# A reduction to tridiagonal form on one core: the gate ahead of the matrix product, the norm behind the panel factor, filled pauses, and direct products for 3-tile steps

## What is computed

```python
deg = jnp.sum(A, axis=0) + jnp.sum(A, axis=1) - jnp.diagonal(A)
d_inv_sqrt = jnp.where(deg > 0, jax.lax.rsqrt(deg), 0.0)
L_norm = d_inv_sqrt[:, None] * (jnp.diag(deg) - A) * d_inv_sqrt[None, :]
_, U = jnp.linalg.eigh(L_norm)
agg = jnp.einsum('mn,bnd->bmd', U.T, features)
h = jax.nn.relu(agg @ W1 + b1)
return jnp.einsum('nm,bmd->bnd', U, h @ W2 + b2)
```

## Time and profile before

| | us |
|---|---|
| median of 3 runs | 4991.18 (4988.99 to 4991.94) |
| the profiled execution | 4989.5 |
| its span, first to last instruction | 4987.7 |
| DVE busy | 4026.5 (81%) |
| PE busy | 2551.1 (51%) |
| ACT busy | 1139.3 (23%) |
| POOL busy | 284.9 (6%) |
| the 510 reduction steps, first reciprocal to last | 55.0 to 2527.7 |

### The profile page before, as it was taken

One profiled execution on the slowest core, in us unless ns is written; L12 is line 12 of the kernel. 1 busy time (PEld: TensorE's weight loads), 2 busy tenths in 40 slices (PEclk: granted clock), 3 DMA queues, 4 the chain that ended last, 5 costly groups with the idle time before them and its releaser, 6 DMA issues.

```text
span 4987.7 us, 116618 instructions
## 1 busy us (share of the span) xinstructions
PE 2551.1 (51%) x40168; PEld 1721.1 (35%) x40168; DVE 4026.5 (81%) x24921; ACT 1139.3 (23%) x5016; POOL 284.9 (6%) x1424
## 2 busy tenths in 40 slices
PE   4666666555556666544457645657423223135048
PEld 3444444444445555433322212322122223124024
DVE  7666666777777888888889999999967897988956
ACT  1212222222223333333311143333210200301001
POOL 1111111111110000000000000000000000000000
PEclk6555555555555555555567767778755555557579
DMA  2000000000000000000000000000000000000001
GB/s 69 2 2 2 2 2 2 2 2 2 2 2 3 4 4 4 3 3 2 3 1 1 1 1 1 1 1 1 1 1 0 0 0 0 0 0 1 0 0 34
DMA packets 20961, 20.11 MB, mean 4 GB/s; under 512 B 6544, under 2 KB 16784, under 8 KB 20368
## 3 DMA queue, kind: packets, MB, share of 16 engines
q1 hardware_dynamic: 20368, 12.65, 0.9%
HBM read 8.41 MB, written 4.20 MB: 3 GB/s over the span
## 4 chain that ended last, share of the span: by engine, by line
DVE 68%; PE 21%; issue 7%; ACT 2%; SPq 0%; DVEq 0%; DMA 0%; POOL 0%
PE bank L622 10%; DVE qp L1437 2%; DVE hid L1096 2%; DVE dif L1799 2%; PE bank L593 2%; PE bank L617 2%; DVE pcol L1076 2%; DVE tau_row L1084 2%; DVE qp L1424 2%; DVE gated L1082 2%; DVE ts L1040 1%; DVE yz L1055 1%; ACT ts L358 1%; DVE hid L1085 1%; PE bank L783 1%
## 5 line engine op out<-in xcount | busy, mean ns | idle before, releaser
L622 PE MATMUL bank<-lapw,hid 128*32 128x160 f32 (+3 forms) x10200 | 660.0, 420 | 81.5 <-DVE lapw L1105 58.3
L622 PEld LDWEIGHTS bank<-lapw,hid 128*32 128x32 f32 x10200 | 394.3, 162 | 200.0 <-DVE lapw L1105 79.7
L700 PE MATMUL bank<-hid,rows 128*128 128x512 f32 (+1 forms) x504 | 320.1, 802 | 275.3 <-ACT dif L410 271.9
L586 PE MATMUL bank<-xp,ones 128*32 128x1 f32 x4080 | 146.0, 202 | 458.1 <-DVE xp L1070 240.6
L371 ACT ACTIVATE swap<-vcols 128x4 f32<-128x4 f32 (+3 forms) x510 | 105.7, 207 | 1049.4 <-DVE xp L1070 696.8
L1050 DVE TENSOR_TENSOR yz<-bank,pick 128x128 f32<-128x128 f32 (+3 forms) x510 | 117.6, 231 | 233.7 <-PE bank L622 233.5
L700 PEld LDWEIGHTS bank<-hid,rows 128*128 128x128 f32 x504 | 118.7, 242 | 468.1 <-ACT dif L410 297.2
L586 PEld LDWEIGHTS bank<-xp,ones 128*32 128x32 f32 x4080 | 102.6, 140 | 501.4 <-DVE xp L1070 262.2
L593 PE MATMUL bank<-ycol,vcols 128*32 128x1 f32 x3064 | 89.8, 199 | 236.3 <-DVE ycol L1061 236.3
L593 PE MATMUL bank<-hid 128*32 128x1 f32 x3064 | 89.8, 199 | 191.6 <-DVE hid L1096 191.6
L586 PE MATMUL bank<-xn,ones 128*32 128x2 f32 x4080 | 141.2, 198 | 84.1 <-DVE xn L1009 84.1
(11 more groups left out here) (761 smaller groups left out, 8268.9 us busy)
## 6 DMA issues: line engine op xcount, KB each, us to landing
out_x<-xs SPq DMA_DIRECT2D x16, 256.0 KB, 2.5
lapw<-in_adj SPq DMA_DIRECT2D x1, 1024.0 KB, 5.3
bias_rows<-in_L_gnn_bg SPq DMA_DIRECT2D x8, 64.0 KB, 5.8
hid<-pair SPq DMA_DIRECT2D x32, 1.0 KB, 1.7
bias_rows<-in_L_gnn_b SPq DMA_DIRECT2D x4, 64.0 KB, 5.7
wg<-in_L_gnn_Wg SPq DMA_DIRECT2D x2, 64.0 KB, 4.8
wg<-in_L_gnn_W SPq DMA_DIRECT2D x2, 64.0 KB, 4.3
dif<-in_L_gnn_Wih SPq DMA_DIRECT2D x1, 0.5 KB, 7.1
```

The source lines that it names most:

```text
L586: m = pe.matmul(into[32 * q:32 * q + 32, :], weights, column, start=True, stop=True)
L622: m = pe.matmul(bank[1][32 * q:32 * q + 32, 0:(T + 1) * 32].rearrange("p (u i) -> p u i", i=32), acols[:, t, k:k + 1].to_broadcast([P, 32] ...
L700: m = pe.matmul(bank[4 * h + q][:, 0:cols_], wih_t[:, p - 1, q * P:(q + 1) * P], hid[:, b0:b0 + nb, t:t + (nw - 1) * p + 1:p], start=True, ...
```

## The change

Two predicates take the place of one. `gated_early(k)` holds for T of 4 and 3, `direct(k)` for T of 3, 2 and 1.

- **T of 4 and 3**: POOL's tail goes to PE in the middle of y, behind its second live tile, and no longer behind y. DVE computes the gate, `gated`, `tau_row`, `scrow` and `ats` ahead of its wait for y, and no longer behind `a1`. The factor (L1103 of before) comes ahead of the norm pair of the next step; the pair comes between the factor and the panel write, and raises one semaphore once instead of twice.
- **T of 3**: v.y and v.p are direct products on PE, 12 each, and the two reduces on DVE go.
- **T of 1**: the strips (and the slots) are issued in the pauses behind the pivot's factor and ahead of v.
- **All direct products**: the loops in `product` change places, the tile outside and the quarter inside.
- The wait for the pivot's value stands behind the reciprocal, and `pcol` has a semaphore of its own, for which ACT's `w0` and DVE's `bcol_` wait.

The diff, cut to its core:

```diff
-def dots(k):
-    return NT - (k + 1) // P <= DOT_TILES
+def gated_early(k):
+    return NT - (k + 1) // P >= 3
+
+
+def direct(k):
+    return NT - (k + 1) // P <= 3
...
@@ ACT
+                act.wait_ge(pcol_ready, k + 1)
                 act.activation(w0[:, t0:], pcol[:, t0:], ACT.Copy, scale=tau_row[:, k:k + 1]).then_inc(w0_ready, 1)
...
@@ PE
-                for q in range(4):
-                    for t in range(T):
+                for t in range(T):
+                    for q in range(4):
                         m = pe.matmul(into[32 * q:32 * q + 32, :], left[:, t:t + 1].to_broadcast([P, 32]), right[:, t:t + 1], start=(t == 0), stop=(t == T - 1))
...
+                    if t == t0 + 1 and early:
+                        pe.wait_ge(tail_in, k + 1)
+                        everywhere(bank[4][:, 0:1], ones[:, 0:32], xn[:, 2:3]).then_inc(tail_ps, 1)
                 m.then_inc(y_done, 1)
...
+                pe.wait_ge(x_ready, k + 1)
+                if direct(k):
                     product(bank[3][:, 0:1], vcols[:, t0:, k], ycol[:, t0:]).then_inc(vy_ps, 1)
-                    pe.wait_ge(x2_ready, k + 1)
+                    pe.wait_ge(pcol_ready, k + 1)
                     product(bank[2][:, 4 * NB:4 * NB + 1], vcols[:, t0:, k], pcol[:, t0:]).then_inc(vp_ps, 1)
...
@@ DVE
                 a = put(V.tensor_scalar(ts[:, 4:5], ts[:, 3:4], bank[0][:, 0:1], ts[:, 0:1], ALU.mult, ALU.add))
+                if T == 1:
+                    z = strips()
                 after(a)
                 a = put(V.tensor_tensor(pair[:, k, 0:1], ts[:, 4:5], ts[:, 1:2], ALU.mult))
                 b = put(V.scalar_tensor_tensor(pair[:, k, 1:2], ts[:, 4:5], ts[:, 1:2], alpha, ALU.mult, ALU.add))
+                if T == 1 and j:
+                    c = slots()
...
+                if early:
+                    dve.wait_ge(tail_ps, k + 1)
+                    g = put(V.tensor_scalar(gate_row[:, k:k + 1], bank[4][:, 0:1], 1e-24, -1.0, ALU.is_gt, ALU.mult))
+                    after(g)
+                    g = put(V.tensor_scalar(gated[:], inv[:], gate_row[:, k:k + 1], None, ALU.mult))
+                    after(g)
+                    V.tensor_tensor(tau_row[:, k:k + 1], gated[:, 0:1], gated[:, 1:2], ALU.mult).then_inc(p_ready, 1)
+                    dve.wait_ge(p_ready, k + 1)
+                    g = put(V.tensor_scalar(scrow[:, k:k + 1], tau_row[:, k:k + 1], gated[:, 0:1], -1.0, ALU.mult, ALU.mult))
+                    after(g)
+                    put(V.scalar_tensor_tensor(ats[:, t0:], a_, scrow[:, k:k + 1], ltm[:, t0:, k + 1], ALU.mult, ALU.mult))
+                if T > 1:
+                    z = strips()
+                    if j:
+                        c = slots()
+                after(z)
+                y = V.tensor_reduce(ycol[:, t0:], yz[:, t0:, 0:32 + 2 * j], AX.X, ALU.add)
...
-                dve.wait_ge(norm_ps, k + 1)
-                if k + 1 < STEPS and not dots(k + 1):
-                    norms(k + 1)
                 dve.wait_ge(vp_ps, k + 1)
                 dve.wait_ge(w0_ready, k + 1)
-                half = ts[:, 7:8] if dots(k) else tau_row[:, k:k + 1]
+                half = ts[:, 7:8] if direct(k) else tau_row[:, k:k + 1]
                 a = put(V.tensor_scalar(ts[:, 6:7], bank[2][:, 4 * NB:4 * NB + 1], tau_row[:, k:k + 1], half, ALU.mult, ALU.mult))
+                if gated_early(k + 1):
+                    dve.wait_ge(norm_ps, k + 1)
+                    norms(k + 1)
                 after(a)
```

More of the change, by code:

```diff
@@ L1024, in _ @@
                 v, a_ = vcols[:, t0:, k], acols[:, t0:, k]
[L1025 removed]
+                early = gated_early(k)
+                alpha = bank[0][:, 1:2] if early else bank[5][:, 0:1]
                 if j == 0 and k:
@@ L1043, in _ @@
                 b = put(V.scalar_tensor_tensor(pair[:, k, 1:2], ts[:, 4:5], ts[:, 1:2], alpha, ALU.mult, ALU.add))
+                if T == 1 and j:
+                    c = slots()
                 after(a)
-                vdone = put(V.scalar_tensor_tensor(v, onehot[:, t0:, k + 1], pair[:, k, 0:1], a_, ALU.mult, ALU.add))
+                put(V.scalar_tensor_tensor(v, onehot[:, t0:, k + 1], pair[:, k, 0:1], a_, ALU.mult, ALU.add))
                 after(b)
-                put(V.reciprocal(inv[:], pair[:, k, :]))
@@ L1059, in _ @@
-                after(a)
-                if dots(k):
-                    V.tensor_reduce(ycol[:, t0:], yz[:, t0:, 0:32 + 2 * j], AX.X, ALU.add).then_inc(x_ready, 1)
+                d = put(V.reciprocal(inv[:], pair[:, k, :]))
+                if early:
+                    dve.wait_ge(tail_ps, k + 1)
[8 more added lines that the diff above has]
+                    put(V.scalar_tensor_tensor(ats[:, t0:], a_, scrow[:, k:k + 1], ltm[:, t0:, k + 1], ALU.mult, ALU.mult))
@@ L1075, in _ @@
                     dve.wait_ge(w0_ready, k)
-                p = V.scalar_tensor_tensor(pcol[:, t0:], a1[:, t0:], pair[:, k, 0:1], ycol[:, t0:], ALU.mult, ALU.add)
-                if dots(k):
-                    p.then_inc(x2_ready, 1)
-                else:
-                    put(p)
-                after(g)
-                g = put(V.tensor_scalar(gated[:], inv[:], gate_row[:, k:k + 1], None, ALU.mult))
-                after(g)
-                V.tensor_tensor(tau_row[:, k:k + 1], gated[:, 0:1], gated[:, 1:2], ALU.mult).then_inc(p_ready, 1)
@@ L1085, in _ @@
-                b = put(V.scalar_tensor_tensor(bcol_[:, t0:, k + 1], pcol[:, t0:], gated[:, 0:1], a1[:, t0:], ALU.mult, ALU.add))
-                dve.wait_ge(p_ready, k + 1)
-                c = put(V.tensor_scalar(scrow[:, k:k + 1], tau_row[:, k:k + 1], gated[:, 0:1], -1.0, ALU.mult, ALU.mult))
+                V.scalar_tensor_tensor(pcol[:, t0:], a1[:, t0:], pair[:, k, 0:1], ycol[:, t0:], ALU.mult, ALU.add).then_inc(pcol_ready, 1)
+                if not early:
+                    after(max(d, g))
+                    g = put(V.tensor_scalar(gated[:], inv[:], gate_row[:, k:k + 1], None, ALU.mult))
+                    after(g)
+                    V.tensor_tensor(tau_row[:, k:k + 1], gated[:, 0:1], gated[:, 1:2], ALU.mult).then_inc(p_ready, 1)
@@ new lines, in _ @@
+                dve.wait_ge(pcol_ready, k + 1)
+                b = put(V.scalar_tensor_tensor(bcol_[:, t0:, k + 1], pcol[:, t0:], gated[:, 0:1], a1[:, t0:], ALU.mult, ALU.add))
+                if not early:
+                    dve.wait_ge(p_ready, k + 1)
+                    c = put(V.tensor_scalar(scrow[:, k:k + 1], tau_row[:, k:k + 1], gated[:, 0:1], -1.0, ALU.mult, ALU.mult))
+                if not direct(k):
+                    V.tensor_tensor_reduce(jcol[:, 2, t0:], v, pcol[:, t0:], 0.5, 0.0, ALU.mult, ALU.add, xp[:, 1:2]).then_inc(x2_ready, 1)
@@ L1088, in _ @@
                 after(b)
                 b = put(V.tensor_tensor(bm[:, t0:], bcol_[:, t0:, k + 1], ltm[:, t0:, k + 1], ALU.mult))
-                after(c)
-                c = put(V.scalar_tensor_tensor(ats[:, t0:], a_, scrow[:, k:k + 1], ltm[:, t0:, k + 1], ALU.mult, ALU.mult))
-                if not dots(k):
-                    V.tensor_tensor_reduce(jcol[:, 2, t0:], v, pcol[:, t0:], 0.5, 0.0, ALU.mult, ALU.add, xp[:, 1:2]).then_inc(x2_ready, 1)
-                after(c)
+                if not early:
+                    after(c)
+                    b = put(V.scalar_tensor_tensor(ats[:, t0:], a_, scrow[:, k:k + 1], ltm[:, t0:, k + 1], ALU.mult, ALU.mult))
```

93 lines of the change are left out of this document (47 added, 46 removed).

## The result

The changed kernel takes 4873.4 us (median) against 4991.6: the ratio is 0.9766, with a 95% interval of 0.9747 to 0.9785. The median is of three executions; a fourth, with a granted clock of 1.0 where the three had 0.60, took 6751.4 us and is left out. I had said 4936, between 4908 and 4962. The sign was right. The size was not: 118 us are saved where 54.5 were forecast. The profiled execution took 4878.2 us.

The account below looks back on a forecast made before the run. The prediction took 510 serial reduction steps to bound the kernel, with DVE holding 68% of the chain of waits. Its terms by tile count, -58 + 19 + 0 - 15.5 = -54.5 us, gave 4936 us, range 4908 to 4962.

Parts of the forecast that it names:

- Parts 1, 2 and 4: Forecasts by live tiles: 4 tiles 58 us saved, 3 tiles 19 us lost, 1 tile 15.5 us saved by filled pauses.
- F to P: From the panel slot's factor (F) to the panel write (P), with the norm pair between; forecast .43 us.
- Part 3: 2-tile steps: DVE order unchanged, only product loops turned; 0 us, bounds +6 to -15 us.
- Rival (b): Turned loops overlap quarters: 2-tile norm product .42 to .29 (15 us), 3-tile factor earlier (9 us); 4912 us, chance .09.
- Part 1: 4-tile steps: .62 us gained behind y, .14 lost to the inserted tail, gate chain hidden; 58 us saved.
- S to A: From the first DVE operation on y (S) to the next column (A); forecast 1.66 us (4 tiles), 1.55 (3 tiles).
- A to F: From the next column (A) to the panel slot's factor (F); forecast .25 us (4 tiles), .21 (3 tiles).
- Y to S: From the start of y (Y) to DVE's first operation on it (S); forecast 2.57 us (4 tiles), 2.38 (3 tiles).
- Part 2: 3-tile steps: .66 us gained behind y, .80 lost because the gate chain ends after y; 19 us lost.
- (d): Rival: the gate chain hides under y with 3 tiles too, each such step 4.21 us; 4852 us, chance .05.
- (e): Rival: the tail's result comes only with y's end, so the gate chain stands behind y; about 5120 us, chance .04.
- (a): Rival: the inserted tail drains PE, y resuming only when it is done, +.27 us per 4-tile step; 4970 us, chance .08.

Follow-up runs that it names:

- e1: Changed kernel, except that the factor operation again waits for the sign operation and not only for the reciprocal: 4894.0 us.
- e2: Kernel before, with one edit: the factor operation waits for the reciprocal alone and not for the sign operation too: 4976.8 us.
- e11: Kernel before, with direct products for the norm, v.y and v.p in 3-tile steps too, and the product loops turned round: 4924.1 us.
- e12: Kernel before, with direct products for the norm, v.y and v.p in 3-tile steps too, but the old loop order (quarter outside): 4970.3 us.
- e5: Changed kernel, with the early gate in 4-tile steps alone; 3-tile steps run like 2-tile ones, without the norm pair on DVE: 4812.2 us.
- e4: Changed kernel without the filled pauses: in 1-tile steps the strips and slots come behind the inverse again: 4894.9 us.
- e7: Changed kernel, with the norm pair ahead of the panel factor again in 4- and 3-tile steps: 4942.2 us.
- e10: Changed kernel, with the early gate alone undone for 4 and 3 tiles: tail product behind y, gate to ats behind a1: 4858.3 us.
- e8: Changed kernel, with v.y and v.p of the 3-tile steps reduced on DVE again: 4879.1 us.

## Why the prediction missed

The chance of .95 for faster stood; the forecast's own case was too pessimistic in all four stages. The mechanisms of Parts 1, 2 and 4 held; what failed are two entries of the sum. The first is a wait and a loop order that were put at nothing: Part 3's **0** measured 13.1 us, and the same wait is missing from Parts 2 and 4. The second is the price of the norm pair behind the factor in Parts 1 and 2: F to P was put at .43 and measured .345 (4 tiles) and .352 (3 tiles) in steps of the width that I had read.

| stage | forecast | measured | what the step missed |
|---|---|---|---|
| 4 tiles | -58 | -75.2 | norm pair, y, panels |
| 3 tiles | +19 | +2.1 | norm pair, wait edit, second product |
| 2 tiles | 0 | -13.1 | wait edit 6.2, loops 5.9 |
| 1 tile | -15.5 | -27.9 | wait edit 5.8, pause .175 for .13 |

**An edit that I read and did not cost (18 of the 60 us that the four stages are off).** Part 3 says that "the DVE order is the same as before for these steps". The order is, the waits aren't: `after(a)` names another operation. The rule for its price stood in the prediction, among the three rates: an independent operation starts .08 before the end of the one ahead, a dependent one .03 to .04 after it. Here L1038's duration of .14 lay between the two. e1 and e2 show it, and that it was free of charge wherever y ended last.

**The loop order (6 us).** Part 3 took 0 with a bound of -.12; it was -.05 with 2 tiles. Rival (b) was right in kind there and less than half its size (6 us for 15). With 3 tiles the turned order is worth .49 a step in the changed kernel, but against a kernel that never was: the old order was not used with 3 tiles before. So it doesn't show in the comparison of the two kernels. By e11 and e12 the direct products of 3-tile steps pay with the old order too, but only a third as much (19.8 us for 59.3).

**The norm pair (the largest part of the rest with 4 tiles).** Part 1 took .23 from L1008 to L1103, and F to P as .43. It is .359. In the earlier trace rows the pair stood directly behind a column that it depended on; behind the factor the first of the two lasts .15 instead of .18 and the second follows it .07 later instead of .11. And the panel write now starts together with the pair's last record, where the factor came .04 behind it. A to P gained .281 on average, where my walk gave .20. Its other terms held: S to A -.424 (forecast -.42), A to F .254 (.25), S on y and not on ats. y grew by .107, not .14 (4 us).

**The 3-tile stage.** I had walked a step in which the panel holds 7 columns. At that width (medians of eight steps) the step takes 4.69 after and 4.73 before: it got .04 shorter, where the walk made it .14 longer. Y to S is 2.346 (said 2.38), the wait edit of .055 less .02 that the walk had too tight. S to A is 1.543 (1.55), A to F .169 (.21, the wait for the second product), F to P .352 (.43, the norm pair), P to Y .283 (.30). Over 120 steps this is 21 us, more than the whole loss that was forecast. What brings the stage back to +2.1 is something that the walk of a single step couldn't show: from step 130 on every fourth 3-tile step of the changed kernel is .27 longer than its neighbours, some 8 us. Before, 15 steps are longer in this way, without this regularity, 4 us. The sign that I had named for a wrong reading of the gate chain, a step shorter than 4.73, came at this width and doesn't mean that: gate to S took 1.02 (said 1.05), and it is the other terms that were too long. The verdict on this stage, that the chain behind inv gives back what S to P gains, holds in the main: the stage takes as long as before, and e5 shows what lay there, 62 us.

**Panel steps.** PE's transposes start .91 after P instead of .63, so w's copy does come .28 later (said .32). Part 1 charged the whole of it. But the two steps around a panel update gain 1.06 with 4 tiles, and two others 1.21: only half of it is paid, 1 us of the stage. With 3 tiles the two steps do .16 worse than two others, as Part 2 had it.

**The rivals.** (d), the gate chain hidden with 3 tiles too, falls: S follows ats at .14. (e), the tail's result held back, falls: in the 4-tile step shown the gate started at Y+1.43 (1.44 forecast). (a) falls too: y grew by .107, not by .41.

What stays open: why three small matmuls in a row into one quarter cost so much more than two (that cost is shown, its mechanism isn't), and what makes every fourth 3-tile step long.

## What to carry to other kernels

When a dependent chain is moved ahead of a product in order to hide it, add up the chain from its last input to the product's end, for each size: with 4 tiles the chain of about 1.05 us fitted under y, with 3 it didn't, and the same move won 34 us and lost 49. Read each wait in a diff for the instruction that it names, not only for its place; a wait that names one operation earlier is worth its successor's duration less the overlap (here .14 less .08, measured .055), at every step that nothing else covers. And let consecutive small matmuls go to different quarters of the columns before judging whether direct products pay. Last, read more than one step: the one that I had read could not show that some steps of a stage are longer than others.

## What the runs showed of the hardware

- Matmuls of 32 columns by 1: 8, 16 and 24 records last .29, .39 and .50 us when the quarter changes with each matmul; with the same quarter 2 or 3 times in a row 16 last .42 and 24 last .85. The 24 records start .013 us apart on average in the first case and .029 in the second. The granted clock over the 510 steps is 0.50 in both kernels, the lower of the two levels (1.2 GHz); the page's row of the changed one, with the 510 steps in its first 20 slices:

```profile
PEclk6555555555555555555577768779655556557579
```

- The Trainium skill (TensorE: Matmul & The Clock Gate, "Why this matters for your kernels") says that outputs in distinct column groups let small matmuls run concurrently. The .50 against .85 for 24 records agrees with it; the .39 against .42 for 16 alone hardly shows it.
- The Trainium skill (VectorE: DVE Perf Modes, "The DRAIN you can't avoid") says that a next operation waits for an empty pipe, and adds that one that is not held starts earlier. The prediction left the second half out. Here the strips started .20 into an operation of .28, and the fill was worth 20 us of the 1-tile stage, so the trace agrees with the second half.
- In the 3-tile stage of the changed kernel every fourth step, from step 130 on, is longer than its neighbours. From step 146 on DVE pauses next to the factor in these steps, and the profile shows nothing that it waited for: in steps 146 to 174 ahead of the factor (A to F about .4 instead of .2), later between the factor and the panel write (F to P up to .72, where the steps between have .34 to .38), which is why the mean of F to P is .405. The 3-tile step shown above is one of them:

```profile
1035.66 0.28 DVE L1133 TENSOR_SCALAR ts<-bank,tau_row,ts 128x1 f32<-128x1 f32 x1 [0.20 <-issue]
```

  The pattern is there in e1, e4, e7 and e10, and gone in e5 and e8, that is without the norm pair or without the direct products in these steps. What causes it was not tried.
